# A graph network's kernel on one core: two reformulations, and new orders for three engines

## The chip, the core and the metric

The kernel runs on one core of a Trainium2 chip. A core has a matrix engine (TensorE, PE), three engines that work on 128 partitions at a time (VectorE, DVE; ScalarE, ACT; GpSimd, POOL) and SyncE (SP), which issues DMAs. They run side by side and wait for each other by semaphores; each takes its own instructions strictly in the order in which they were written. The metric is the device time of one execution in microseconds (us), as the median of several runs.

## What is computed

64 graphs of 128 nodes with 64 features; `adj` holds 0 and 1, with a self-loop at each node. Four layers follow one another, each with a residual and a layer norm:

```python
x = _layernorm(x + _L0_gnn_ref(x, adj, ...))   # PNA: mean, max, min, std over neighbours
x = _layernorm(x + _L1_gnn_ref(x, adj, ...))   # adj @ (x @ W) + bias
x = _layernorm(x + _L2_gnn_ref(x, adj, ...))   # weighted quantiles of the neighbours, then an MLP
x = _layernorm(x + _L3_gnn_ref(x, adj))        # (A @ x) / rowsum(A), A = adj + I
```

The parts that matter here:

```python
h_mod = h_cat @ W_pre + b_pre              # L0: a part of the node itself plus a part of the neighbour
mean = s1 / deg_safe
var = jax.nn.relu(s2 / deg_safe - mean * mean)
std = jnp.sqrt(var + EPS)
...
skip = jnp.where(m > T_THRESH, (m + K_DIL - 1) // K_DIL, 1)   # L2: drops some edges of rich nodes
sv = jnp.sort(vals, axis=2)                # L2: the neighbours' values, sorted for each feature
return y * mask[..., None].astype(dtp)     # L2; the mask is all ones in the inputs
...
num = jnp.einsum('bij,bjd->bid', A, nodes) # L3
denom = jnp.sum(A, axis=2, keepdims=True)
```

## The kernel before

The 64 graphs go through in eight groups of eight (`Turn`, `t.n` = 0 to 7). All steps of a group are small functions, each for one engine. What sets the order is written out by hand: TENSOR_ORDER, SCALAR_ORDER and VECTOR_ORDER are lists of entries `step:part@lag`, and `pipeline` goes through the list once per turn of the pipeline and runs each entry for group (turn + lag). So `so:0-20@-1` is the first 20 steps of the sort of the group before. In one turn up to three groups are at work, at different layers; with lags from -2 to 2 the loop makes ten turns that hold something, and the first and last hold little. A step starts when its semaphores (`s[...]`) allow it, and all that is queued behind it on its engine waits with it.

The steps of a group, in the order of the data (PE, ACT, DVE or POOL in brackets):

- Sorting the nodes of a graph by degree: `cm`, `gt`, `P` (DVE, P is a permutation matrix), `kc`, `lv` (PE). Permuting: `yr`, `ap`, `xt` (PE), evicted by `ysb`, `adj`, `xs` (ACT). `pb` copies P to bf16.
- `sm` (PE) fetches by P a table of per-node factors (`rows`, `rowsb`), and `rw` (DVE) adds up its three bf16 parts into `rowP`: 1/deg, deg/deg, two log-degree factors, 1/(deg+1) and 1 more, the mask. `kn`, `sk`, `dr`, `dt`, `dtc`, `va`, `vt`, `p1`, `k1`, `p2`, `k2`, `cr`, `sg` find which edges L2 drops, and number each node's neighbours (`key1` for L0, `key2` for L2).
- L0: `qp` (PE) makes the neighbour's part of `h_mod` in one half of PSUM tile `pna` and the node's own part in the other. `qo`, `pm`, `pl` (ACT) with `q1`, `q2` (PE) split the first into three bf16 parts, `ng` (DVE) negates them. `rp` and `up` (ACT) scale the node's own part by two factors, one instruction per graph each. `ss` (PE) multiplies by `adjP`, `ac` (ACT) scales by 1/deg. `me` (DVE) gives the mean with the node's part, `we` (DVE) the variance in four passes, `sd` the root, `mt` and `mts` a transpose. `h0` (DVE) makes one-hot matrices, `g0:0` to `g0:7` (PE) gather neighbours with them into a ring of two PSUM banks, `e0` (ACT) moves them out to `slot0`, `tr` (DVE) takes maxima and minima. `yl` (PE), `ys` (ACT), `zf` (DVE) make the layer's sum, and `n0q`, `n0d`, `n0r`, `n0x` the norm: squares (ACT), their sum (DVE), a root (ACT), the scaling (DVE). `n1..`, `n2..`, `n3..` do the same for the other layers.
- L1: `b1`, `b1e`, `b2`, `z1`, norm, result `x2`. `b3`, `b3e` transpose it.
- L2: `xh`, `xm`, `xl` (ACT) and `r1`, `r2` (DVE) split `x2` into three bf16 parts, `parts2`. `h2` (DVE) makes one-hot matrices, `g2:0` to `g2:3` (PE) gather through the same ring, `e2` (ACT) moves out to `slot2`. `so` (DVE) is a sorting network of 66 steps of minimum and maximum on `slot2` and `swap` (which the profile calls `hot`). `wr` (PE) makes the weights of the ranks, `wg` and `ag` (DVE) weigh and add the ranks; `c2` (PE), `c2e` (ACT), `c3` (PE) are the MLP, `y2e` (ACT) scales by the mask, graph by graph, `z2` (DVE) adds `x2`.
- L3: `c6` (PE) multiplies by `adjP`, `z3e` (ACT) scales by 1/(deg+1), `xr` (ACT) scales x3, `z3` (DVE) adds, and `sc` (POOL) scatters the rows to DRAM in eight indirect DMAs.

`pre` steps run once, in the first turns: degrees and factors, the weights, the tables, the rank weights. Where inputs are unusual, a slow general branch runs behind everything; with these inputs it does not.

Norms, matmuls and scalings all go through the helpers at L442, L445, L839 and L1440 to L1445, so many steps share these lines in the profile.

## Time and profile before

| | |
|---|---|
| median of 3 runs | 649.8 us (649.49 to 651.43) |
| the profiled execution | 646.34 us, its span 644.8 us |
| busy: VectorE | 514.6 us (80%) |
| busy: TensorE | 482.3 us (75%) |
| busy: ScalarE | 370.4 us (57%) |
| busy: GpSimd | 112.8 us (17%) |
| moved by DMA | 15.48 MB read, 2.10 MB written |

The shares are means over a start, five or six turns that repeat exactly, and an end in which little overlaps. A turn is best read by itself. In the timeline, a row is a start time, a length, an engine, a line of the kernel, and output and input by their names in the program; brackets give the idle time before it and whose work ended it.

### The profile page before, as it was taken

Reading aid. Unit: us, or ns where it says so; the run is one execution under the profiler, and the core shown is the slowest. Engines: PE = TensorE matmul, PEld = TensorE weight load, DVE = VectorE, ACT = ScalarE, POOL = GpSimd, SP = SyncE. Lnnn points to the kernel's source line nnn. Section 1 sums busy time; section 2 is a strip of 40 time slices with the busy share of each in tenths; the row PEclk is TensorE's granted clock in tenths of the full one; section 3 lists DMA queues with packets and bytes.
Section 4 is the critical chain, followed back from the end, with each engine's and each line's share of the span. In section 5 each row is a group of like instructions: output and inputs, shape, how many; then the busy total and the mean of one; then the engine's idle time right before and its main releaser. Section 6 shows DMA issues by size and latency. Waiting matters only on the chain.

```text
span 644.8 us, 10421 instructions
## 1 busy us (share of the span) xinstructions
PE 482.3 (75%) x3380; PEld 320.0 (50%) x3419; DVE 514.6 (80%) x1504; ACT 370.4 (57%) x990; POOL 112.8 (17%) x186
## 2 busy tenths in 40 slices
PE   2467968797988889798979897989888977861420
PEld 2443655365545655475557554755575545440220
DVE  4895639999799978999899989997999799379220
ACT  0264677447874678568855885588558842440230
POOL 4300010301014100510061006100610070006022
PEclk9866998999899989989998999899989997555555
DMA  8400020002000200020002000200000000000000
GB/s 312 162 0 1 2 82 1 2 1 82 2 4 16 81 2 2 17 83 2 2 16 83 2 1 18 83 2 1 17 2 2 2 17 2 1 0 17 0 6 15
DMA packets 6718, 18.32 MB, mean 28 GB/s; under 512 B 1792, under 2 KB 1920, under 8 KB 6144
## 3 DMA queue, kind: packets, MB, share of 16 engines
q1 hardware_dynamic: 4608, 15.48, 6.8%
q0 software_dynamic: 2048, 2.10, 1.1%
q8 instruction: 28, 0.46, 0.3%
q14 instruction: 34, 0.28, 0.1%
HBM read 15.48 MB, written 2.10 MB: 27 GB/s over the span
## 4 chain that ended last, share of the span: by engine, by line
DVE 34%; issue 27%; PE 22%; ACT 8%; POOL 6%; POOLq 0%; DVEq 0%; ACTq 0%
DVE hot L1479 7%; DVE slot L1479 7%; PE pna L445 6%; DVE slot L1404 5%; PE pna L442 5%; POOL out_dram L1099 5%; PE ring L442 4%; PE relab L442 2%; PE rest L442 2%; DVE deg L1143 1%; ACT wv L863 1%; PE ring L655 1%; DVE slot L1502 1%; DVE P L1309 1%; DVE hot L1492 1%
## 5 line engine op out<-in xcount | busy, mean ns | idle before, releaser
L442 PE MATMUL ring<-hot,parts 128*64 128x384 bf16 (+3 forms) x753 | 137.1, 358 | 0.9
L1099 POOL DMA_INDIRECT out_dram<-xo,idx x64 | 78.1, 1220 | 309.9 <-DVE xo L1445 292.9
L912 ACT ACTIVATE slot<-ring 128x512 f32<-128x512 f32 (+1 forms) x128 | 61.6, 525 | 42.6 <-PE ring L442 38.4
L442 PEld LDWEIGHTS ring<-hot,parts 128*128 128x128 bf16 (+1 forms) x768 | 55.5, 107 | 39.6 <-issue 4.1
L863 ACT ACTIVATE wv<-pna,rowP 128x64 f32<-128x64 f32 x128 | 28.0, 329 | 77.6 <-PE pna L442 77.6
L1404 DVE TENSOR_TENSOR slot<-slot 128x128 f32<-128x128 f32 (+2 forms) x144 | 53.1, 424 | 2.8 <-ACT slot L912 0.9
L1479 DVE TENSOR_TENSOR hot<-slot 128x64 f32<-128x64 f32 (+5 forms) x136 | 50.8, 407 | 3.5 <-ACT slot L921 3.5
L445 PE MATMUL ring<-emp,rowsel 112*128 112x512 bf16 (+1 forms) x128 | 45.3, 354 | 10.9 <-ACT slot L912 7.0
L1479 DVE TENSOR_TENSOR slot<-slot 128x64 f32<-128x64 f32 (+5 forms) x136 | 51.2, 406 | 0.0
L445 PE MATMUL pna<-bdx,xT 128*128 128x384 f32 x64 | 28.6, 530 | 16.5 <-DVE zF L1436 16.5
L921 ACT ACTIVATE slot<-ring 128x384 f32<-128x384 f32 x64 | 31.3, 502 | 15.3 <-PE ring L442 15.2
L442 PE MATMUL pna<-weights,QQ 128*128 128x192 f32 x128 | 36.6, 371 | 0.0
L445 PE MATMUL rest<-x2T,weights 128*128 128x512 f32 x32 | 22.3, 785 | 18.1 <-DVE x2T L1506 10.4
L442 PE MATMUL pna<-wmm,slot 128*128 128x192 f32 x128 | 34.5, 354 | 0.0
L1479 DVE TENSOR_TENSOR hot<-hot 128x128 f32<-128x128 f32 (+3 forms) x96 | 33.6, 378 | 0.0
L1085 POOL TENSOR_SCALAR skp<-dcol 128x2 f32<-128x2 f32 x8 | 2.1, 264 | 175.7 <-ACT dcol L780 175.7
L839 ACT ACTIVATE zB<-rest,rowP 128x64 f32<-128x64 f32 x128 | 28.0, 340 | 6.9 <-PE rest L442 4.0
L445 PE MATMUL ring<-sgnT,delta 32*128 32x512 bf16 (+2 forms) x48 | 14.6, 364 | 22.4 <-DVE slot L1492 20.3
L1479 DVE TENSOR_TENSOR slot<-hot 128x64 f32<-128x64 f32 (+5 forms) x88 | 31.3, 378 | 0.0
L1440 DVE TENSOR_REDUCE stB<-sqB 128x8 f32<-128x512 f32 x16 | 10.9, 683 | 25.2 <-ACT sqB L926 25.2
L445 PEld LDWEIGHTS ring<-emp,rowsel 112*128 112x128 bf16 x128 | 12.9, 101 | 33.8 <-ACT slot L912 22.2
L839 ACT ACTIVATE m<-pna,rowP 128x64 f32<-128x64 f32 x128 | 28.7, 394 | 0.1
(280 smaller groups left out, 1139.1 us busy)
## 6 DMA issues: line engine op xcount, KB each, us to landing
Cc<-adj_cols_dram SPq DMA_DIRECT2D x8, 512.0 KB, 3.8
R<-adj_rows_dram SPq DMA_DIRECT2D x8, 512.0 KB, 5.4
slot<-adj_rows_dram SPq DMA_DIRECT2D x4, 1024.0 KB, 12.4
xn<-x_nat_dram SPq DMA_DIRECT2D x8, 256.0 KB, 5.5
out_dram<-xo,idx POOLq DMA_INDIRECT x64
weights<-wpack_dram SPq DMA_DIRECT2D x1, 608.5 KB, 8.0
biasr<-wrows_dram SPq DMA_DIRECT2D x1, 128.0 KB, 9.4
own_loop<-adj_diag_dram SPq DMA_DIRECT2D x1, 32.0 KB, 15.1
```

Of the source, the lines that this page charges most:

```text
L442: return mm(*a, start=False, stop=True, skip_group_check=True, **k)
L445: return mm(*a, start=True, stop=True, skip_group_check=True, **k)
L655: mm(ps[:, OFF2[k] - lo:OFF2[k] - lo + CAP2[k]], fill2[:, k, :, :].rearrange("p a d -> p (a d)"), sgnT[t.n % KEEP][:, c, 0:CAP2[k]], start ...
L839: last = A(dst[:, g, :], src(g), ACT.Copy, scale=rowP[t.n % ROWKEEP][:, g, which:which + 1])
L863: last = A(ys[:, g, f, :], PQ[:, 256 * g + D * (f + 1):256 * g + D * (f + 2)], ACT.Copy, scale=rowP[t.n % ROWKEEP][:, 4 * h + g, AMP + f:A ...
L912: A(slot0[:, g, lo:hi], PG[ring["g0", t.n, 2 * g + j][0]][:, 0:hi - lo], ACT.Copy).then_inc(s["slot0"], 1)
L921: A(slot2[:, c, lo:hi], PG[ring["g2", t.n, 2 * c + j][0]][:, 0:hi - lo], ACT.Copy).then_inc(s["slot2"], 1)
L1099: nc.gpsimd.indirect_dma_start(out=out, out_offset=bass.IndirectOffsetOnAxis(ap=idx[t.n % ROWKEEP][:, g:g + 1], axis=0), in_=xo[:, g, :], ...
L1143: own(V.tensor_reduce(deg[:, k * CHUNK:(k + 1) * CHUNK], chunk[k], AX.X, ALU.add))
L1404: return V.tensor_tensor(dst, dst, src, ALU.max)
L1440: V.tensor_reduce(st[:, 0, :], sq[:, :, :], AX.X, ALU.add).then_inc(s[signal], 1)
L1479: mark(("sort", k), V.tensor_tensor(low if is_min else wire(b, 1 - sb_, width), low, high, ALU.min if is_min else ALU.max))
```

## The change

First reformulation, L0: the variance of `h_mod` over the neighbours does not depend on the node's own part. So in the normal path `qp` makes the neighbours' part only, `rp`, `up` and `me` are gone, and `we` is one subtraction. The own part of mean and maxima reaches the result through the weights `bdx`, which get one more product (`x_weights`, once). The mask goes the same way: `y2e` is gone, the one-column products with `maskb` in `sm` are gone, and an incomplete mask counts as unusual.

Second reformulation: L3 is multiplied by (deg + 1), which a norm cancels if its epsilon is scaled too: `z3e` is gone, `xr` scales by deg + 2, and `n3d` adds a correction `EPS3` to the sum of squares. `z2_` and `z3_` read PSUM directly. The table of factors has five columns where it had eight. And the three parts of `x2` are no longer rounded but cut: the upper 16 bits of each f32 word are used in place as bf16, at a step of two elements (`upper`), so `xh`, `xm`, `xl` are gone and `r1`, `r2` write `less[0]`, `less[1]`.

Third, the three orders are new. The list of VectorE is turned round, so that a turn begins with `wg:1`; most new lags come from that. Really moved are: steps 0 to 47 of the sort stand together; `z3` and `n3d`, `n3x` come late in the turn, with `c6` as `c6@-3` in TensorE's next turn; `va` and `p2` no longer stand between the `g2`; `rank_weights` (`pre:3`) comes after the degrees (`pre:4`); `adj` and `xs` end ScalarE's turn, `ac` comes before `e2:0`.

```diff
-INV, RATIO, AMP, ATT, RDEN, MASK, RDEN1, UNRATIO = range(8)
-NF = 8
-ROWW = 3 * NF + 1
+INV, AMP, ATT, DEG2, EPS3 = range(5)
+RATIO, UNRATIO, RDEN, RDEN1, MASK = range(3, 8)
+NF, GENERAL_NF = 5, 8
+ROWW, GENERAL_ROWW = 3 * NF + 1, 3 * GENERAL_NF + 1
+DEG_MAX = 1.0e9
...
-    g0:1@-1 cr@-1 g0:2@-1 g0:3@-1 kc@0 g0:4@-1 lv@0 g0:5@-1 g0:6@-1 g0:7@-1 yl:0@-1 wr:0@-2 wr:1@-2 yr@0 yl:1@-1
...
+    g0:1@-1 c6@-3 g0:2@-1 cr@-1 g0:3@-1 kc@0 g0:4@-1 g0:5@-1 g0:6@-1 lv@0 g0:7@-1 yl:0@-1 wr:0@-2 b3@-2 yr@0
...
-    adj@0 n0q@-1 xs@0 n0r@-1 kn@0 b3e@-2 qo@0 up@0 b1e@-1 rp@0 n1q@-1 c2e:0@-2 pm@0 n1r@-1 k1@0 xh@-1 pl@0
...
+    n0r@-1 qo@0 b1e@-1 kn@0 pm@0 c2e:0@-2 pl@0 n1q@-1 n1r@-1 c2e:1@-2 k1@0 ac@0 e2:0@-1 n2q@-2 e2:1@-1
...
-    zf:1@-1 wg:2@-2 nb@0 n0d@-1 wg:3@-2 pre:1@0 mp@0 n0x@-1 rw@0 wg:4@-2 wg:5@-2 ag@-2 z1@-1 dr@0 n1d@-1
...
+    h0:11-13@0 pre:4@0 pre:6@-2 cm@1 pre:3@0 so:0-47@-1 gt@1 so:47-50@-1 tr:0@0 so:50-53@-1 P@1 tr:1@0 z3@-2
...
+        def upper(words):
+            return words[:, :, :].bitcast(BF16).rearrange("p g (d two) -> p g d two", two=2)[:, :, :, 1]
+
+        def parts2(t):
+            return [upper(w) for w in (x2[t.n % 2], less[0], less[1])]
...
                 last.then_inc(s["q_ps"], 1)
-                for c in range(PAIRS):
-                    last = new(cols(bank(PQ, 1), c), xT[:, c, :], bdqp[:, 128:256])
-                last.then_inc(s["p_ps"], 1)
+                if not t.fast:
+                    for c in range(PAIRS):
+                        last = new(cols(bank(PQ, 1), c), xT[:, c, :], bdqp[:, 128:256])
...
-                            done = add(ps[64 * a:64 * a + 64, 0:hi - lo], parts2[:, 2 * c + a, part, :],
+                            done = add(ps[64 * a:64 * a + 64, 0:hi - lo], parts2(t)[part][:, 2 * c + a, :],
                                        hot2[:, 2 * c + a, lo:hi])
...
+            def x_weights(t):
+
+                pe.wait_ge(wdve, 1)
+                if t.fast:
+                    mm(PZ[:, 0:3 * D], wat, flat(raw[:, 6:9, :]), start=True, stop=False)
+                    mm(PZ[:, 0:3 * D], wat[0:64, :], flat(raw[0:64, 3:6, :]), start=False, stop=True).then_inc(vps, 1)
+                else:
+                    mm(PZ[:, 0:3 * D], wat, flat(raw[:, 6:9, :]), start=True, stop=True).then_inc(vps, 1)
...
-            def xh(t):
-                act.wait_ge(s["x2"], given(t))
-                before(act, "g2_ps", t, 1, 2 * PAIRS)
-                A(parts2[:, :, 0, :], x2[t.n % 2][:, :, :], ACT.Copy).then_inc(s["xh"], 1)
-
-            def xm(t):
-                act.wait_ge(s["xd1"], given(t))
-                A(parts2[:, :, 1, :], rest[:, :, :], ACT.Copy).then_inc(s["xm"], 1)
-
-            def xl(t):
-                act.wait_ge(s["xd2"], given(t))
-                A(parts2[:, :, 2, :], rest[:, :, :], ACT.Copy).then_inc(s["parts2"], 1)
-
             def c2e(t, a):
...
             def we(t):
 
                 dve.wait_ge(s["acs"], given(t))
-                dve.wait_ge(s["up"], given(t))
-                before(dve, "std", t)
-                dve.wait_ge(s["mean"], given(t))
+                if t.fast:
+                    before(dve, "std", t)
+                    dve.wait_ge(s["asq"], given(t))
+                    V.tensor_tensor(wv[:, :, :], QQ[:, :, 1, :], sqF[:, :, :], ALU.subtract).then_inc(s["vv"], 1)
+                    return
+                dve.wait_ge(s["up"], late(t))
+                dve.wait_ge(s["mean"], late(t))
                 own(V.tensor_tensor(wv[:, :, :], m4[:, :, 0, :], QQ[:, :, 0, :], ALU.add))
                 own(V.tensor_tensor(wv[:, :, :], wv[:, :, :], up, ALU.mult))
                 own(V.tensor_tensor(wv[:, :, :], wv[:, :, :], QQ[:, :, 1, :], ALU.add))
...
             def r1(t):
-                dve.wait_ge(s["xh"], given(t))
-                before(dve, "parts2", t)
-                V.tensor_tensor(rest[:, :, :], x2[t.n % 2][:, :, :], parts2[:, :, 0, :], ALU.subtract).then_inc(s["xd1"], 1)
+                before(dve, "g2_ps", t, 1, 2 * PAIRS)
+                dve.wait_ge(s["x2"], given(t))
+                V.tensor_tensor(less[0][:, :, :], x2[t.n % 2][:, :, :], upper(x2[t.n % 2]), ALU.subtract).then_inc(s["xd1"], 1)
 
             def r2(t):
-                dve.wait_ge(s["xm"], given(t))
                 dve.wait_ge(s["xd1"], given(t))
-                V.tensor_tensor(rest[:, :, :], rest[:, :, :], parts2[:, :, 1, :], ALU.subtract).then_inc(s["xd2"], 1)
+                V.tensor_tensor(less[1][:, :, :], less[0][:, :, :], upper(less[0]), ALU.subtract).then_inc(s["parts2"], 1)
 
             def z2_(t):
-                dve.wait_ge(s["y2s"], given(t))
                 dve.wait_ge(s["x2"], given(t))
+                if t.fast:
+                    dve.wait_ge(s["y2_ps"], given(t))
+                    before(dve, "sq3", t)
+                    V.tensor_tensor(flat(zB[:, :, :]), PZ[:, 512:1024], flat(x2[t.n % 2][:, :, :]),
+                                    ALU.add).then_inc(s["z2"], 1)
+                    return
+                dve.wait_ge(s["y2s"], late(t))
...
             def z3_(t):
-                dve.wait_ge(s["z3s"], given(t))
                 dve.wait_ge(s["xr"], given(t))
+                if t.fast:
+                    dve.wait_ge(s["z3_ps"], given(t))
+                    V.tensor_tensor(flat(zB[:, :, :]), PZ[:, 512:1024], flat(xr[:, :, :]),
+                                    ALU.add).then_inc(s["z3"], 1)
+                    return
+                dve.wait_ge(s["z3s"], late(t))
                 V.tensor_tensor(zB[:, :, :], zB[:, :, :], xr[:, :, :], ALU.add).then_inc(s["z3"], 1)
 
             def n3d(t):
-                summed(t, stB, sqB, "sq3", "rd3")
+                if not t.fast:
+                    summed(t, stB, sqB, "sq3", "rd3")
+                    return
+                dve.wait_ge(s["sq3"], given(t))
+                own(V.tensor_reduce(stB[:, 0, :], sqB[:, :, :], AX.X, ALU.add))
+                V.tensor_tensor(stB[:, 0, :], stB[:, 0, :], row_of(t)[:, :, EPS3], ALU.add).then_inc(s["rd3"], 1)
 
```

TensorE, a middle turn, from the second bank of `g2:0` on (`fill` and `hot,parts` are `g2`, `maskP`, `dts` and `Pb` are `va`). Before:

```order
L442 MATMUL ring<-hot,parts 64x424 x6
L445 MATMUL relab<-maskP,identb 128x512
L442 MATMUL relab<-dts,Pb 128x32
L442 MATMUL relab<-Pb,dts 32x128
...
L655 MATMUL ring<-sgnT,fill 128x128 x3
L442 MATMUL ring<-hot,parts 64x384 x6
```

The same place now, and the end of `g2:3` further on:

```order
L456 MATMUL ring<-hot,less 64x424 x4
L676 MATMUL ring<-sgnT,fill 128x128 x3
L456 MATMUL ring<-hot,x_0 64x384 x2
...
L459 MATMUL relab<-identb,drop 128x128 x2
L459 MATMUL ring<-emp,rowsel 128x512
L456 MATMUL ring<-hot,parts 128x512 x3
L459 MATMUL ring<-emp,rowsel 128x328
L456 MATMUL ring<-hot,parts 128x328 x3
L459 MATMUL relab<-maskP,identb 128x512
```

`g2:1` follows `g2:0` at once, and `va` comes behind `dt` and `g0:0`.

ScalarE, a middle turn, from `ac` (QQ, then sqF) on; `slot<-ring` are the evictions `e2`, `zB` is `y2e`. Before:

```order
L887 ACTIVATE QQ<-pna,rowP 128x128 x8
L892 ACTIVATE sqF<-QQ 128x512
L921 ACTIVATE slot<-ring 128x384
L921 ACTIVATE slot<-ring 128x424
L839 ACTIVATE zB<-rest,rowP 128x64 x8
L796 ACTIVATE validT<-relab 128x1024
```

And now:

```order
L817 ACTIVATE key<-relab,not_member 128x1024
L914 ACTIVATE QQ<-pna,rowP 128x128 x8
L919 ACTIVATE sqF<-QQ 128x512
L948 ACTIVATE slot<-ring 128x384
L948 ACTIVATE slot<-ring 128x424
L953 ACTIVATE sqB<-zB 128x512
L948 ACTIVATE slot<-ring 128x384
L948 ACTIVATE slot<-ring 128x424
L957 ACTIVATE stB<-stB,eps 128x8
```

`y2e` and `vt` are gone from between the evictions, `n2q` (sqB) and `n2r` (stB) have moved up there.

VectorE, a middle turn, from the end of `ag` (x2T) on. Before:

```order
L1506 TENSOR_TENSOR x2T<-x2T,slot 128x512
L1457 TENSOR_TENSOR zF<-rest,x 128x512
L1344 TENSOR_SCALAR drop<-keyN,skp 128x128 x2
L1348 SCALAR_TENSOR_TENSOR drop<-keyN,skp,drop 128x128 x2
L1440 TENSOR_REDUCE stF<-sqF 128x8
```

That place in the turn shows this in the changed kernel:

```order
L1541 TENSOR_TENSOR x2T<-x2T,slot 128x512
L1353 TENSOR_SCALAR maskP<-adjP 128x1024
L1401 TENSOR_SCALAR hot<-key_0 128x8x128
L1363 TENSOR_REDUCE rowP<-relab 128x40
L1365 COPY nkS<-relab 112x1
L1366 TENSOR_TENSOR idx<-relab,base 128x8
L1401 TENSOR_SCALAR hot<-key_0 128x8x128 x2
L1492 TENSOR_TENSOR zF<-rest,x 128x512
```

`mp`, `rw` and the first one-hot matrices stand between `ag` and `z1`.

## Rows read from the trace of the kernel before

**Rows 1.** Busy time by stretch: start and end, length, engines, PEclk, DMA share, GB/s.

```profile
330.50:395.39 64.89, 55.89 (x424) 37.52 (x428) 59.17 (x171) 45.06 (x123) 11.92 (x18) 0.97 0.08 26
```

**Rows 2.** Timeline of VectorE in that turn: start, us, engine, line, operation.

```profile
330.50 1.22 DVE L1309 TENSOR_TENSOR P<-place,placed 128x1024 f32<-128x1024 f32 x1
...
345.98 0.42 DVE L1435 TENSOR_TENSOR zF<-pna,wv 128x256 f32<-128x256 f32 x1 [0.49 <-ACT wv L863]
...
351.29 0.72 DVE L1492 TENSOR_TENSOR hot<-hot,ring 128x288 f32<-128x288 f32 x2 [0.41 <-PE ring L445]
...
355.55 0.69 DVE L1506 TENSOR_TENSOR x2T<-x2T,slot 128x512 f32<-128x512 f32 x1
...
373.81 0.69 DVE L1440 TENSOR_REDUCE stB<-sqB 128x8 f32<-128x512 f32 x1 [3.61 <-ACT sqB L926]
...
376.76 0.22 DVE L1479 TENSOR_TENSOR hot<-slot 128x64 f32<-128x64 f32 x1
```

**Rows 3.** Timeline of TensorE in that turn: c2, c2, ss, g2, va, g2, c6.

```profile
356.30 1.13 PE L445 MATMUL rest<-x2T,weights 128*128 128x512 f32 x2 [0.94 <-DVE x2T L1506]
358.40 1.10 PE L445 MATMUL rest<-x2T,weights 128*128 128x512 f32 x2 [0.98 <-ACT hT L984]
...
360.98 2.05 PE L445 MATMUL pna<-QQ,adjP 128*128 128x128 f32 x16 [0.82 <-ACT parts L835]
...
364.92 0.34 PE L655 MATMUL ring<-sgnT,fill 32*128 32x128 bf16 x3
...
366.79 0.39 PE L445 MATMUL relab<-maskP,identb 128*128 128x512 bf16 x1
...
369.48 0.34 PE L655 MATMUL ring<-sgnT,fill 32*128 32x128 bf16 x3
...
376.08 2.00 PE L445 MATMUL rest<-x,adjP 128*128 128x64 f32 x16
```

**Rows 4.** Timeline of ScalarE in that turn: ac, and the last eviction of g2.

```profile
363.32 2.16 ACT L887 ACTIVATE QQ<-pna,rowP 128x128 f32<-128x128 f32 x8
...
375.74 0.98 ACT L921 ACTIVATE slot<-ring 128x384 f32<-128x384 f32 x2
```

**Rows 5.** Groups over the run: busy us, mean ns, idle before.

```profile
L839 ACT ACTIVATE m<-pna,rowP 128x64 f32<-128x64 f32 x128 | 28.7, 394 | 0.1
...
L839 ACT ACTIVATE zB<-rest,rowP 128x64 f32<-128x64 f32 x128 | 28.0, 340 | 6.9 <-PE rest L442 4.0 <-PE rest L445 2.9
...
L445 PE MATMUL pna<-weights,xT 128*128 128x128 f32 x64 | 9.3, 293 | 0.0
...
L1391 DVE TENSOR_TENSOR wv<-wv,m 128x512 f32<-128x512 f32 x8 | 5.5, 692 | 0.3
```

**Rows 6.** Groups by form, weight loads of TensorE with 64 columns.

```profile
L442 PEld LDWEIGHTS ring<-hot,parts 128*64 128x64 bf16 x384 | 17.2, 114 | 9.0 <-issue 1.5 <-DVE hot L1370 0.2
...
L445 PEld LDWEIGHTS rest<-adjP,x 128*64 128x64 f32 x128 | 7.5, 147 | 1.3 <-DVE x L1445 1.0
```

**Rows 7.** Timeline of the start, VectorE three times (rank_weights, h0, sort), TensorE (g0:1).

```profile
38.98 0.29 DVE L1263 TENSOR_SCALAR zB<-steps_of 32x2 f32<-32x2 f32 x3
...
42.88 2.33 DVE L1362 TENSOR_SCALAR hot<-key 128x1024 bf16<-128x1024 bf16 x9
...
57.84 0.39 PE L445 MATMUL ring<-emp,rowsel 112*128 112x512 bf16 x1 [2.98 <-ACT slot L912]
...
114.33 0.91 DVE L1479 TENSOR_TENSOR hot<-slot 128x64 f32<-128x64 f32 x1 [1.13 <-ACT slot L921]
```

**Rows 8.** Timeline of the end: two sorts begin, c6 of TensorE, z3e of ScalarE.

```profile
506.52 0.23 DVE L1479 TENSOR_TENSOR hot<-slot 128x64 f32<-128x64 f32 x1 [0.36 <-ACT slot L921]
...
569.32 3.68 PE L445 MATMUL rest<-x,adjP 128*128 128x64 f32 x16
...
569.99 0.23 DVE L1479 TENSOR_TENSOR hot<-slot 128x64 f32<-128x64 f32 x1 [2.01 <-ACT slot L921]
...
618.58 1.75 ACT L839 ACTIVATE zB<-rest,rowP 128x64 f32<-128x64 f32 x8 [1.72 <-PE rest L445]
```

193 lines of the change are left out of this document (112 added, 81 removed).

## The prediction

> **What bounds the kernel now.** First the busy time by engine in one turn of the pipeline [rows 1]: of 64.89 us VectorE is busy for 59.17, TensorE for 55.89, ScalarE for 45.06. VectorE is the bound, but it stands still for 5.7 us of each turn, so the next question is where. Its own instructions in order of time [rows 2] answer that: 3.61 us before the reduction of `sqB` at 373.81, 0.49 before `zF`, 0.41 before the weighting at 351.29, and small change of some 0.1 us each. The 3.61 us lie in one stretch. It begins when `ag` has finished (355.55 and 0.69, so 356.24) and ends with the first step of the sort at 376.76: 20.52 us, in which VectorE works for 16.9.
>
> What fills the 20.52 us is seen on TensorE and ScalarE [rows 3, 4]. `c2` starts at 356.30 and again at 358.40, `ss` (the product with `adjP`) runs from 360.98, `c3` behind it, `g2:0` starts at 364.92. The four `g2` would take 1.87 each, but `va` stands between the first two from 366.79 to 369.48, and the last ends at 376.08. ScalarE moves its last half out at 375.74 to 376.72, and the sort starts. So the critical path runs through ag, c2, ss, c3, g2 with va in it, and the evictions, and back to VectorE.
>
> **Change, part 1: work taken away.** ScalarE, per graph group: `rp` and `up` are 16 instructions of the 128 that take 28.7 us, so 3.6 us; `y2e` and `z3e` are the 128 that take 28.0 us, 3.5 us [rows 5]; the three casts `xh`, `xm`, `xl` some 0.6 each (the size of a 512-wide pass), 1.8 us. ScalarE falls from 45.06 to some 36.2 us. It is not the bound, and 28 us of the turn cover it; this pays only where its queue held others up.
>
> VectorE: `me` goes and so do three of the four passes of `we`. One pass is 0.69 alone [rows 5], 0.60 behind another one, and 0.72 where it waits for its own predecessor: 0.60 + 3 x 0.72 = 2.76 us off. `rw` is narrower, 0.1 off. Added: `n3d` gets one 128x8 addition and a wait on its own reduction, 0.25 on. `z2_` and `z3_` now read PSUM where they read `zB`; nothing in the rows prices a PSUM operand apart, so between nothing and 0.1 each; I take nothing. Sum: 2.6 us.
>
> TensorE: the second half of `qp` goes, 9.3 us for 64 instructions, 1.16 with overlap, 1.0 net [rows 5], and eight one-column products with `maskb`, some 0.1. From 55.89 to some 54.7 us. The one matmul that `x_weights` adds runs once, below 1 us.
>
> `parts2` is now the upper half of each f32 word of `x2` and `less`, so the weights of `g2` are bf16 at a step of two elements. No row shows such a load. The nearest from below is the packed 64-column bf16 load, 114 ns; from above the 64-column f32 load, 147 ns [rows 6]. Below zero is excluded, since the same number of columns is loaded. There are 48 such loads per turn: 0 to 48 x 0.033 = 1.6 us, all on the path above. I take 0, since the matmuls behind these loads hide part of them. The Trainium skill ("SBUF — State Buffer", the note on cachelines) says that bf16 can be read at a step within a 16-byte line without loss if a line serves at least two reads; by it the price is 0 too, and no run here shows it yet. VectorE reads the same strided halves in `r1` and `r2`; before, it read bf16 there as well, so no change.
>
> **Change, part 2: the new orders.** In the stretch from ag to sort, counted from the end of ag: VectorE keeps its 16.9 us of work, less 2.76, plus `mp` and `rw` that moved in behind `ag` (0.6 and 0.5), less some small waits: 15.0 us. The path of TensorE: `c2:0` 1.16; `c2e:0` is hidden behind `q2` and `p1`, which now stand between the two `c2`, so that `c2:1` starts at 2.2 and ends at 3.3; `ss` then takes 2.05 (to 5.4), and `c3` 1.85 (to 7.25) (360.98 to 364.92 for both [rows 3]). `c3` needs `c2e:1`, which ScalarE now issues only behind `n1q` and `n1r`, so behind z1 and n1d on VectorE: 5.1, just in time. `g2:0` starts at 7.25 and ends at 9.1. Here the order costs something: `ac` (8 scalings and a square, 2.7 us, [rows 4]) stands ahead of `e2:0`, and starts behind `k1` at 6.05, so the first eviction comes at 8.8 and `g2:1` waits 0.2. Then `n2q` (0.6) and `n2r` stand between evictions; `n2r` waits for `n2d` on VectorE, at 12.5, while the ring has but two banks. The four `g2` end at 15.2 and not at 14.7, the last eviction at 15.7. `va`, `mt` and `p2` are gone from between the `g2` and come behind `g0:0`, where TensorE has 4 us of slack per turn. So the stretch falls from 20.5 to 15.7, and VectorE still waits 0.7 us in it.
>
> The rest of the turn was 64.89 - 20.52 = 44.4 us, with 0.9 of waits [rows 2]. Less `mp` and `rw` 1.1, plus 0.25, less 0.1, it is 42.6 without waits. The sort now runs in one piece of 47 steps with nothing in it, then alternates with `gt`, `tr`, `P`, `z3`, `zf`. Followed one by one, what VectorE meets there: `kc` is done about 0.3 us before `gt`; `lv` 1.2 before `P`; the last `e0` 4 before `tr:1`; `ys:0` 0.6 before `zf:0`; `ys:1`, which now stands behind `n3r` and so behind `n3d`, 0.9 before `zf:1`. No big wait, but thin margins; I put 0.6 us for them, within the 0 to 0.9 that such waits cost before. A turn is then 42.6 + 0.6 + 15.7 = 58.9 us.
>
> **Sum over the run.** The sorts start at 114.33 for the first group, at 376.76 for the fifth, 506.52 for the seventh and 569.99 for the last [rows 2, 7, 8]. From the first to the fifth that is 65.6 per turn, later 64.88: the early turns are a little longer, and on the mean of six, 65.37, 0.5 above the steady one. I take 0.3 for it: 59.2 x 6 = 355.2.
> Start: `g0:1` begins at 57.84 [rows 7], held by ScalarE's first eviction, which waits for the degrees of the later graphs. `rank_weights`, 38.98 to 42.88, now comes behind those degrees, and 2.8 us of `me` and `we` are gone; TensorE then has its own work (`va`, `mt`, `p2` at a low clock) until some 53.5, so 4.3 us come off. The half turn that follows, from the end of the second `zf` (345.98 and its two passes, 346.8 [rows 2]) to the sort, falls from 30.0 to 23: 9.4 to 7.2 for the part up to ag, since `nb`, `mp`, `rw` and a weighting lie elsewhere, and 20.5 to 15.7. First sort: 114.3 - 4.3 - 7.0 = 103.
> The last interval was 63.5 us, with TensorE at half clock [rows 8], and its path (ag, c2, c3, g2) has neither `va` nor `ss` in it before or after: 63.5 kept.
> End: 644.8 - 569.99 = 74.8 us from the last sort, one chain without overlap. In it `y2e` and `z3e`, 1.75 us each [rows 8], are gone, 0.25 is added: 71.5. `c6` and `z3` a turn later add nothing there, since nothing else is left to do.
> 103 + 355.2 + 63.5 + 71.5 = 593.2 us of span, with the 1.5 around it 594.7 for a profiled execution (646.3 before). The median of the runs lies 0.54% above the profiled one (649.8 to 646.34): 597.9, so 598.
>
> **Rivals.**
> *A, VectorE without waits.* If the evictions keep up better than I walked, the stretch is VectorE's own 15.0 and the thin margins hold: 57.6 + 0.3 per turn, so 8 us less and up to 4 at the start: 586. For it: the walk adds waits of ScalarE's queue one behind another. Against: the order `ac` ahead of `e2:0` is fixed.
> *B, strided weights cost.* 1.6 us per turn on the path, times 8: 598 + 13 = 611. For it: f32 loads of the same width take 147 against 114 ns. Against: loads overlap matmuls (PEld is busy 37.5 of 64.9 us).
> *C, the order gives less than it says.* If the thin margins fail (a late `ys:1`, `gt` or `P`), half of the waits come back at another place. With all the waits that were (4.5 us) the turn is 59.2 - 2.6 + 0.7 + 4.5 = 61.8: 598 + 6 x 2.9 = 615; nothing but the removed work counts then.
> *D, slower.* One mechanism: TensorE's clock. Over the steady turn the granted clock is 0.97 [rows 1]; in the last 100 us the records show the lower level, 1.2 GHz, and the same 16 instructions of `c6` take 3.68 where they took 2.00 [rows 3, 8]. If the new order left pauses in which the clock falls, TensorE's 54.7 us would grow by up to 0.84 of themselves; slower than before begins where more than a quarter of its work is at the lower level (54.7 x 1.21 = 66). All at that level would be 100 us a turn, 850 us. Against: TensorE will be busy for 93% of the turn, more than now.
>
> **Chances.** The forecast (590 to 606) 0.55, A 0.15, B 0.10, C 0.16, D 0.02, and 0.02 that it all cancels within 0.3%, which is about what a measurement of this kernel can tell from no change. Faster by over 0.3%: 0.96; same 0.02; slower 0.02. The likeliest is 598. The range takes in A (586) with 2 us below it and C (615) with 2 above: 584 to 617.
>
> **What would show it.** Right: turns of 58.5 to 59.5 us between two sorts; VectorE's wait before the sort under 1.5 us, behind ScalarE's `slot`; ScalarE busy for 36 us of a turn, VectorE for 56.6; first sort near 103; the four `g2` in one run of some 8 us. B shows as weight loads of `parts2` longer than 114 ns, C as new waits before `gt`, `P` or `zf`. The prediction is wrong first if the ring of two banks holds `g2` longer than 8 us, or if the start does not move.

## The result, and the profile after

The changed kernel takes 587.9 us (median of four executions: 579.32, 587.55, 588.17 and 589.48), the kernel before 649.6 us beside it. Every ratio in this document leaves out executions that took over 1.5% more than the fastest one of their kernel, which here leaves 579.32 and 587.55, in the mean 583.4 us. The ratio is 0.898, with a 95% interval of 0.887 to 0.909; in a second measurement it is 0.902 (0.895 to 0.908). The direction was right and the size was not: 52 us were forecast to be saved, the medians save 62, these two executions 66 in the mean and the shortest one 70.

The profiled execution is the one of 589.48 us, the longest of the four. What of it an execution of 579.66 us shows too, and what not, is in the first experiment. These are its stretches: a steady turn, the part of it from the end of `ag` to the sort, the last interval between two sorts, and the end. The columns are the stretch, its length, the busy time (and instructions) of TensorE, its weight loads, VectorE, ScalarE and GpSimd, then the granted clock of TensorE, the share of the DMA engines and GB/s.

```profile
core 0: us, PE busy (x) PEld busy (x) DVE busy (x) ACT busy (x) POOL busy (x), PEclk, DMA share, GB/s
277.11:335.11 58.00, 54.00 (x413) 35.41 (x411) 56.22 (x168) 37.57 (x89) 10.16 (x16) 1.00 0.09 29
319.45:335.11 15.66, 15.14 (x138) 9.12 (x138) 14.52 (x46) 10.96 (x26) 2.96 (x10) 1.00 0.02 6
451.14:516.92 65.78, 56.23 (x307) 33.18 (x305) 47.60 (x137) 27.96 (x68) 7.86 (x8) 0.75 0.02 5
516.92:587.20 70.28, 19.29 (x66) 12.62 (x65) 34.36 (x103) 8.66 (x25) 15.39 (x16) 0.50 0.03 8
```

The turn is 58.00 where it was 64.89 [rows 1]; VectorE is busy for 56.22 us of it. So of the 6.9 us per turn 3.0 are work that VectorE no longer does (59.17 to 56.22) and 3.9 are time in which it no longer stands still (5.7 to 1.8). What it still waits for is seen in its rows in order of time. In one whole turn there is one wait of more than 0.05 us (in brackets, us of idle time and who ended it):

```profile
318.75 0.69 DVE L1541 TENSOR_TENSOR x2T<-x2T,slot 128x512 f32<-128x512 f32 x1
...
333.56 0.69 DVE L1319 TENSOR_SCALAR key<-Cc 128x1024 bf16<-128x1024 f32 x1
335.11 0.23 DVE L1514 TENSOR_TENSOR hot<-slot 128x64 f32<-128x64 f32 x1 [0.86 <-ACT slot L948]
```

The first row is the last pass of `ag`, the third the first step of the sort. The waits of 3.61, 0.49 and 0.41 us [rows 2] are gone; 0.86 is left. TensorE and ScalarE in that stretch, to be laid beside [rows 3, 4]:

```profile
319.50 1.12 PE L459 MATMUL rest<-x2T,weights 128*128 128x512 f32 x2
...
321.61 1.10 PE L459 MATMUL rest<-x2T,weights 128*128 128x512 f32 x2
322.54 1.95 PE L459 MATMUL pna<-QQ,adjP 128*128 128x128 f32 x16
324.43 0.39 PE L459 MATMUL rest<-biasb,rows 128*128 128x512 bf16 x1
...
326.48 0.34 PE L676 MATMUL ring<-sgnT,fill 32*128 32x128 bf16 x3
...
332.56 0.34 PE L676 MATMUL ring<-sgnT,fill 32*128 32x128 bf16 x3 [0.19 <-ACT slot L948]
...
334.45 0.28 PE L459 MATMUL relab<-identb,drop 128*128 128x128 bf16 x2
```

```profile
325.27 2.17 ACT L914 ACTIVATE QQ<-pna,rowP 128x128 f32<-128x128 f32 x8
327.48 0.63 ACT L919 ACTIVATE sqF<-QQ 128x512 f32<-128x512 f32 x1
328.02 0.98 ACT L948 ACTIVATE slot<-ring 128x384 f32<-128x384 f32 x2
...
334.56 0.52 ACT L948 ACTIVATE slot<-ring 128x424 f32<-128x424 f32 x1 [0.51 <-PE ring L456]
```

`c2`, `c2`, `ss`, `c3` follow each other without a pause, the four `g2` run from 326.48 to 334.45 in one piece, and the last half is moved out at 334.56 to 335.08. The stretch is 15.66 us.

### The profile page after: what moved, and what is told of

It reads as the page before. It is cut to its first block, busy times and chain, and to the rows that moved or that the text cites. A ratio compares the mean times of both kernels' runs of the same rounds, so it can differ in the third digit from the quotient of the medians.

```text
span 587.2 us, 9826 instructions
## 1 busy us (share of the span) xinstructions
PE 470.0 (80%) x3293; PEld 305.9 (52%) x3293; DVE 490.4 (84%) x1480; ACT 308.2 (52%) x710; POOL 96.3 (16%) x179
## 4 chain that ended last, share of the span: by engine, by line
issue 63%; POOL 14%; DVE 10%; PE 8%; ACT 2%; POOLq 0%; DVEq 0%; ACTq 0%
POOL out_dram L1115 11%; PE pna L456 2%; PE ring L456 2%; DVE slot L1514 1%; DVE hot L1514 1%; PE pna L459 1%; PE ring L459 1%; ACT wv L892 1%; PE relab L459 1%; DVE hot L1393 1%; DVE slot L1439 1%; PE relab L456 0%; DVE biasb L1228 0%; DVE deg L1157 0%; DVE pcol L1257 0%
## 5 line engine op out<-in xcount | busy, mean ns | idle before, releaser
L1115 POOL DMA_INDIRECT out_dram<-xo,idx x64 | 64.9, 1014 | 353.6 <-DVE xo L1480 336.6
L456 PE MATMUL ring<-hot,parts 128*128 128x512 bf16 (+1 forms) x384 | 90.1, 347 | 0.0
L939 ACT ACTIVATE slot<-ring 128x512 f32<-128x512 f32 (+1 forms) x128 | 62.7, 522 | 36.2 <-PE ring L456 36.1
L456 PEld LDWEIGHTS ring<-hot,parts 128*128 128x128 bf16 x384 | 38.0, 99 | 30.2 <-issue 1.9
L456 PE MATMUL ring<-hot,less 128*64 128x384 bf16 (+1 forms) x256 | 35.5, 360 | 0.0
L456 PE MATMUL pna<-weights,m 128*128 128x192 f32 x128 | 34.4, 351 | 0.0
L456 PE MATMUL pna<-wmm,slot 128*128 128x192 f32 x128 | 32.3, 335 | 0.0
L676 PEld LDWEIGHTS ring<-sgnT,fill 32*128 32x128 bf16 x352 | 16.3, 95 | 25.4 <-ACT slot L948 12.5
L676 PE MATMUL ring<-sgnT,fill 32*128 32x128 bf16 (+5 forms) x352 | 25.1, 198 | 3.9 <-DVE less L1565 2.0
L456 PEld LDWEIGHTS pna<-weights,m 128*128 128x128 f32 x128 | 22.0, 199 | 7.7 <-issue 7.7
```

What stands on the lines that cost most here:

```text
L456: return mm(*a, start=False, stop=True, skip_group_check=True, **k)
L676: mm(ps[:, OFF2[k] - lo:OFF2[k] - lo + CAP2[k]], fill2[:, k, :, :].rearrange("p a d -> p (a d)"), sgnT[t.n % KEEP][:, c, 0:CAP2[k]], start ...
L939: A(slot0[:, g, lo:hi], PG[ring["g0", t.n, 2 * g + j][0]][:, 0:hi - lo], ACT.Copy).then_inc(s["slot0"], 1)
L1115: nc.gpsimd.indirect_dma_start(out=out, out_offset=bass.IndirectOffsetOnAxis(ap=idx[t.n % ROWKEEP][:, g:g + 1], axis=0), in_=xo[:, g, :], ...
```

## Experiments

Each is one edit of the changed kernel; `work_only` has three order tables edited, nearly back to those of the kernel before. "The changed kernel" is 588 us in the median, with turns of 58.0.

**The same kernel again** (after_again).

> The changed kernel itself once more, for its spread: four executions gave 579.32, 587.55, 588.17 and 589.48 us, with mean granted clocks of 0.915, 0.897, 0.894 and 0.886. Theory 1: the spread is TensorE's clock in the last 100 us alone; the turns between the sorts stay at 58.0 us in every execution, and an execution with a clock of 0.91 or more comes out near 579, one with 0.89 near 588. Theory 2: the steady turns differ as well (58.0 against some 57.0), and then an execution near 579 shows first sort and end as in the 587.2 us span. A median between 579 and 588 is expected by both.

Measured: 579.66 to 590.44 us, median 588.3. The profiled execution was one of 579.66:

```profile
217.75:275.74 57.99, 53.50 (x407) 35.42 (x411) 56.22 (x168) 37.54 (x89) 10.14 (x16) 1.00 0.08 28
449.73:507.04 57.31, 47.24 (x307) 29.74 (x308) 47.66 (x138) 27.72 (x68) 8.04 (x8) 0.91 0.02 6
```

The steady turn is the same to 0.01 us, and the end to 0.02 (70.26). The last interval is 57.31 in place of 65.78, with a clock of 0.91 in place of 0.75. That is 8.5 of the 9.9 us between the two spans (587.2 and 577.3); 1.3 more lie ahead of the second sort, which starts at 161.09 and 159.75. Theory 1 holds for most of the spread: it is one interval, in which TensorE's clock holds or does not. Only two executions of this kernel were profiled. A third length is in c6_early and n2_late below, whose turns are those of this kernel too: 63.58 us (in an execution of 586.77) and 63.24 (587.39). The first:

```profile
450.74:514.32 63.58, 53.18 (x303) 31.60 (x306) 47.47 (x138) 27.80 (x68) 8.62 (x8) 0.81 0.02 5
```

**The removed work alone** (work_only). Order tables as in the kernel before, without the steps that are gone. The larger part of ScalarE's:

```
-    ... qo@0 up@0 b1e@-1 rp@0 n1q@-1 ... k1@0 xh@-1 pl@0 c2e:1@-2 xm@-1 dtc@0 xl@-1 ac@0 e2:0@-1 y2e@-2 vt@0 ...
+    ... qo@0 b1e@-1 n1q@-1 ... k1@0 pl@0 c2e:1@-2 dtc@0 ac@0 e2:0@-1 vt@0 ...
```

> Only the removed work: all that the change takes away or reformulates is gone, but the steps of TensorE, ScalarE and VectorE stand in the order of the kernel before. Theory 1 (the orders carry the larger part, as the prediction's sum had it): VectorE's 2.6 us per turn go and part of its 4.5 us of waits stays, since va and p2 still stand between the g2: turns of 61 to 62.3 us, a time of 618 to 628 us. Theory 2 (ScalarE's queue was what held the evictions up, so its 8.9 us free the path by themselves): waits go too, turns of 58.5 to 59.5, 598 to 605 us.

Measured: 636.3 us (ratio 0.981, interval 0.976 to 0.986). Both theories expected more of a saving. Its sorts start at 110.20, 172.06, 240.21, 304.13, 370.41, 434.32, 500.63 and 563.8: 4.1 us less in the start, 0.3 per turn (65.07 in the mean, 65.37 before), 4.3 less in the end. Two of its turns:

```profile
370.41:434.32 63.91, 55.08 (x408) 36.28 (x413) 56.29 (x170) 37.28 (x89) 11.72 (x16) 0.97 0.08 26
434.32:500.63 66.31, 57.41 (x408) 37.47 (x413) 55.86 (x169) 37.40 (x89) 11.72 (x16) 0.92 0.02 5
```

VectorE is busy for 56.3 us as in the changed kernel, ScalarE for 37.3, and from the third on the turns alternate between 64 and 66 (the first two take 61.9 and 68.2). The time is in one wait, which was 3.61 [rows 2] and is 6.24 in the shorter turns and 6.48 in the longer, as here, and in ScalarE's queue ahead of it:

```profile
367.46 0.69 DVE L1477 TENSOR_REDUCE stB<-sqB 128x8 f32<-128x512 f32 x1 [6.48 <-ACT sqB L955]
```

```profile
363.23 1.02 ACT L830 ACTIVATE validT<-relab 128x1024 bf16<-128x1024 f32 x1 [2.16 <-PE relab L458]
...
366.82 0.61 ACT L955 ACTIVATE sqB<-zB 128x512 f32<-128x512 f32 x1
```

`sqB` stands behind `vt` (`validT`), and `vt` waits for `va` on TensorE. VectorE comes 2.6 us earlier to the same door. The turns with the clock of the kernel before, 0.97, are 63.91 where they were 64.89: the removed work is worth 1.0 us there. The others, at 0.92, give it back. Nearly all of their 2.4 us more is in `c2:1` and `ss`. The two `c2` in a short turn, then in a long one:

```profile
284.24 1.13 PE L461 MATMUL rest<-x2T,weights 128*128 128x512 f32 x2 [1.89 <-DVE x2T L1543]
286.35 1.10 PE L461 MATMUL rest<-x2T,weights 128*128 128x512 f32 x2 [0.98 <-ACT hT L1000]
...
348.16 1.23 PE L461 MATMUL rest<-x2T,weights 128*128 128x512 f32 x2 [1.89 <-DVE x2T L1543]
350.37 2.05 PE L461 MATMUL rest<-x2T,weights 128*128 128x512 f32 x2 [0.98 <-ACT hT L1000]
```

The waits are the same to 0.01 us in both turns, and only in the second does the clock fall. So the small saving is the work of the queue and of the clock together.

**va and p2 back between the g2** (va_back).

```
-    ... ss@0 c3@-2 g2:0@-1 g2:1@-1 g2:2@-1 g2:3@-1 dt@0 g0:0@0 va@0 mt@0 p2@0
+    ... ss@0 c3@-2 dt@0 g2:0@-1 va@0 g2:1@-1 p2@0 g2:2@-1 g2:3@-1 g0:0@0 mt@0
-    ... ac@0 e2:0@-1 n2q@-2 e2:1@-1 n2r@-2 e2:2@-1 e2:3@-1 pre:0@2 dtc@0 sd@0 xr@-2 vt@0 ...
+    ... ac@0 dtc@0 e2:0@-1 n2q@-2 vt@0 e2:1@-1 n2r@-2 e2:2@-1 e2:3@-1 pre:0@2 sd@0 xr@-2 ...
```

> The changed kernel with one move undone: va stands again between the first two g2 and p2 between the next two, dt ahead of g2:0, and ScalarE's dtc and vt where they feed them. Theory 1 (the path from ag to the sort is TensorE's): va was 2.7 us there, p2 about 1, so the stretch from ag to the sort grows from 15.6 to 18.5 to 19.5 us, the turn from 58.0 to 61 to 62, the time by 18 to 24 us. Theory 2 (VectorE's work alone sets the turn, and TensorE has slack): under 1 us per turn, within 6 us of the changed kernel.

Measured: 619.31, 625.49, 635.88 and 651.60 us, with mean clocks of 0.887, 0.870, 0.854 and 0.818. Two turns of the execution of 625.49:

```profile
172.61:234.65 62.04, 53.65 (x407) 35.37 (x411) 56.32 (x168) 37.63 (x89) 10.13 (x16) 1.00 0.08 27
234.65:300.49 65.84, 57.29 (x407) 36.18 (x411) 56.35 (x168) 37.74 (x89) 10.15 (x16) 0.92 0.08 25
284.00:291.00 7.00, 5.71 (x42) 2.77 (x42) 5.95 (x20) 3.41 (x9) 0.00 (x0) 0.69 0.00 0
```

At full clock the turn is 62.04, 4.0 more, the top of what theory 1 gave, and the stretch from ag to the sort holds all of it (19.70 us where it was 15.66). The longer turns have the same work at a lower clock, from the first `g2` on, which costs 3.8 us more per turn. The span of 623.3 us is 36 longer than that of the changed kernel, where theory 1 had 18 to 24: 29 lie in the six turns (24 of it at 4.0 each), 10 ahead of the first sort, and the last interval is 3 shorter. Ahead of those `g2`, `dt` waits for VectorE's `drop`, but the rows of a short turn (the first) and of a long one show the same wait:

```profile
223.02 0.27 PE L459 MATMUL relab<-identb,drop 128*128 128x128 bf16 x2 [0.95 <-DVE drop L1379]
...
285.04 0.27 PE L459 MATMUL relab<-identb,drop 128*128 128x128 bf16 x2 [0.95 <-DVE drop L1379]
```

So the wait alone does not tell in which turn the clock falls. The two longest executions were not profiled.

**ac and the norms later on ScalarE** (ac_late), and **the norms alone** (n2_late).

```
-    ... ac@0 e2:0@-1 n2q@-2 e2:1@-1 n2r@-2 e2:2@-1 e2:3@-1 ...
+    ... e2:0@-1 ac@0 e2:1@-1 n2q@-2 e2:2@-1 n2r@-2 e2:3@-1 ...      (ac_late)
+    ... ac@0 e2:0@-1 e2:1@-1 n2q@-2 e2:2@-1 n2r@-2 e2:3@-1 ...      (n2_late)
```

> The changed kernel with ScalarE's ac behind the first eviction of g2 and n2q, n2r one eviction later each. Theory 1 (the prediction's walk: ac ahead of e2:0 and the norms between the evictions make VectorE's last wait, 0.86 us before the sort): the wait falls to 0 to 0.3 us, turns of 57.2 to 57.7, 2 to 5 us less in all. Theory 2 (g2 itself, 1.9 to 2.1 us for each of four, sets the end of the stretch): nothing within 1 us. Theory 3: the weighted mean and deviation come later and hold yl up: 0.5 us or more per turn longer.

> The changed kernel with n2q and n2r one eviction later each on ScalarE; ac stays ahead of the first eviction. It parts the two moves of the run with both, which took 61.2 us per turn: there VectorE waited 2.1 us for the square of ac and 0.4 for the root of n2. Theory 1 (the cost was ac's): turns within 0.3 us of 58.0, the time within 3 us of the changed kernel. Theory 2 (the norms between the evictions are what counts): turns of 59.5 to 61, 9 to 18 us more.

Measured: 609.5 us (ratio 0.942, 0.938 to 0.945) and 587.0 us (0.902, 0.896 to 0.908). With `ac` later the turn is 61.22, theory 3. Its waits:

```profile
340.65 0.69 DVE L1421 TENSOR_TENSOR wv<-QQ,sqF 128x512 f32<-128x512 f32 x1 [2.10 <-ACT sqF L919]
...
343.79 0.20 DVE L1479 RECIPROCAL stB<-stB 128x8 f32<-128x8 f32 x1 [0.41 <-ACT stB L957]
...
346.72 0.23 DVE L1514 TENSOR_TENSOR hot<-slot 128x64 f32<-128x64 f32 x1 [1.00 <-ACT slot L948]
```

VectorE's `we` needs the square behind `ac`; the wait before the sort that the move was to remove grew to 1.00. With the norms alone moved, the wait before the sort is gone, 0.40 and 0.35 us stand before two steps of the norm instead, and the turn is 57.99 as before. So the prediction was right that `ac` ahead of `e2:0` puts the first eviction off (it starts at 328.02, as soon as `ac` is done, without a wait for TensorE), but the price of the other order is higher; and the 0.86 us cannot be had on ScalarE by this shift of the norms.

**VectorE's removed time put back** (dve_back): four passes ahead of `we`.

```
+                    for _ in range(4):
+                        own(V.tensor_tensor(junk[:, :, :], QQ[:, :, 1, :], sqF[:, :, :], ALU.subtract))
                     V.tensor_tensor(wv[:, :, :], QQ[:, :, 1, :], sqF[:, :, :], ALU.subtract).then_inc(s["vv"], 1)
```

> The changed kernel with VectorE's removed time put back where it was, ahead of the pass of we: four passes over 128x512 f32 (no result of theirs is used), each waited for by VectorE itself, some 0.72 us each, 2.9 us per graph group. Theory 1 (with the new orders VectorE's own work is the turn): the 0.86 us of wait before the sort take up a part, the rest goes into the turn: 2.0 to 2.9 us for each of 6 turns and for the first, none in the last interval, so 14 to 20 us more than the changed kernel, turns of 60 to 60.9. Theory 2 (TensorE's path from ag to the sort is the turn): under 1 us per turn, under 7 us in all.

Measured: 615.2 us (ratio 0.948, 0.944 to 0.952), so 27 us more. A turn and the second half of its stretch, and the added passes:

```profile
291.30:352.77 61.47, 55.37 (x413) 35.90 (x412) 59.02 (x173) 37.54 (x89) 10.14 (x16) 0.97 0.08 27
343.00:352.77 9.77, 6.66 (x72) 3.32 (x71) 8.10 (x23) 3.88 (x10) 0.00 (x0) 0.90 0.01 2
```

```profile
343.90 2.86 DVE L1423 TENSOR_TENSOR junk<-QQ,sqF 128x512 f32<-128x512 f32 x4
...
352.77 0.23 DVE L1517 TENSOR_TENSOR hot<-slot 128x64 f32<-128x64 f32 x1 [1.40 <-ACT slot L949]
```

2.86 us of VectorE make the turn 3.47 longer: the size of theory 1, and more than it. But the 0.86 us of wait took nothing up; it grew to 1.40. The way leads through the other two engines:

```profile
348.95 0.30 ACT L958 ACTIVATE stB<-stB,eps 128x8 f32<-128x8 f32 x1 [3.69 <-DVE stB L1478]
...
349.68 0.34 PE L677 MATMUL ring<-sgnT,fill 32*128 32x128 bf16 x3 [3.11 <-ACT slot L949]
```

The first row is `n2r`, which stands between two evictions and now waits 3.69 us for `n2d` on VectorE (0.77 in the changed kernel). The last `g2` waits behind that eviction, 3.11 us where it was 0.19, and starts 16.0 us after the end of `ag` where it was 13.1. That is 2.9 of the 3.5 us. The other 0.5 is the clock, 0.70 from the start of that `g2` to the sort.

**Time put back on ScalarE** (act_back): 16 small copies ahead of n1q, 3 wide ones ahead of ac, 8 small ones behind e2:0 and 8 behind e0:0.

```
-    ... pl@0 n1q@-1 n1r@-1 c2e:1@-2 k1@0 ac@0 e2:0@-1 n2q@-2 ... vt@0 e0:0@0 ...
+    ... pl@0 extra:0@0 n1q@-1 n1r@-1 c2e:1@-2 k1@0 extra:3@0 extra:3@0 extra:3@0 ac@0 e2:0@-1 extra:1@0 n2q@-2
+        ... vt@0 e0:0@0 extra:1@0 ...
```

> The changed kernel with ScalarE's removed time put back near where it was (32 copies of 64 columns and 3 of 512 to a scratch buffer, no result of theirs used): 16 small ones ahead of n1q, the 3 wide ones between k1 and ac, 8 small ones behind e2:0 and 8 behind e0:0; some 8.9 us per graph group. Theory 1 (ScalarE is no bound, its work is covered): under 1 us per turn. Theory 2 (its queue holds up what VectorE waits for, in the place where it stands): 16 ahead of n1q make n1 3.6 us late and so c2e:1, c3 and g2, and the 1.8 us ahead of ac as well: 3 to 6 us per turn, 20 to 40 us in all.

Measured: 638.5 us (ratio 0.983, 0.978 to 0.988), so 50 us more, beyond theory 2. ScalarE is busy for 43.55 us of a turn (6.0 us more, less than the 8.9 put down), far from being the bound, and the turn is 64.79, as long as in the kernel before:

```profile
303.62:368.41 64.79, 58.12 (x413) 36.85 (x412) 56.62 (x169) 43.55 (x124) 10.15 (x16) 0.92 0.08 26
357.00:368.41 11.41, 9.57 (x73) 4.40 (x74) 5.86 (x20) 6.99 (x23) 0.00 (x0) 0.62 0.01 1
```

Three of the added groups stand in the stretch from ag to the sort, with 2.44, 1.95 and 1.27 us, 5.7 together. TensorE's rows show how they become 6.8 us of turn:

```profile
352.89 0.39 PE L460 MATMUL rest<-biasb,rows 128*128 128x512 bf16 x1 [1.88 <-ACT hT L999]
...
358.84 0.34 PE L677 MATMUL ring<-sgnT,fill 32*128 32x128 bf16 x3 [1.95 <-ACT slot L949]
...
361.31 0.49 PE L677 MATMUL ring<-sgnT,fill 32*128 32x128 bf16 x3
...
364.53 0.49 PE L677 MATMUL ring<-sgnT,fill 32*128 32x128 bf16 x3
```

`c3` waits 1.88 us and the second `g2` 1.95 us for ScalarE. Then the clock falls within that `g2`, and the last two take 3.2 us each (361.31 to 364.53 to 367.74) in place of 2.0. Here the waits and the slower products behind them add up.

This run does not have the old work in its old place. In the kernel before, `up` and `rp` ran ahead of the end of `ag` at 356.24 [rows 2], and `n1q` still waited 1.43 us for VectorE behind them:

```profile
351.56 1.76 ACT L839 ACTIVATE m<-pna,rowP 128x64 f32<-128x64 f32 x8
353.61 1.84 ACT L839 ACTIVATE m<-pna,rowP 128x64 f32<-128x64 f32 x8
```

Here the 16 copies start 2.3 us after the end of `ag` (348.25 and 345.97) and hold `n1q` up. So the run prices ScalarE's time in this place of the new order, and does not show what the new orders would give with the old work where it was.

**rank_weights early** (ranks_early).

```
-    ... n1x@-1 h2:8-9@-1 ... pre:6@-2 cm@1 pre:3@0 so:0-47@-1 ...
+    ... n1x@-1 pre:3@0 h2:8-9@-1 ... pre:6@-2 cm@1 so:0-47@-1 ...
```

> The changed kernel with rank_weights (3.9 us of VectorE, once) again ahead of the degrees of the later graphs, everything else as it is. Theory 1 (the start is held by the degrees, which release ScalarE's first eviction): the degrees end at 53.3 in place of 49.4, g0:1 starts at 53.8 to 54.9 in place of 51.0, the first sort some 3 to 3.9 us later, and the time 3 to 4 us longer. Theory 2 (TensorE's own work until 51.0 us holds it in the changed kernel): 2 us or less.

Measured: 592.7 us (ratio 0.912, 0.907 to 0.917), some 4 to 5 us more. ScalarE's first eviction starts at 52.84 where it started at 49.66, and the second `g0` at 54.16 where it started at 50.99, 3.2 later, as theory 1 had it for the step; the first sort is 7 us later (108.05), the second 4.9. The rest of the 7 us lies in 90 to 108 us, where the clock is 0.73 and 0.50 and was 1.00 in the changed kernel:

```profile
90.00:100.00 10.00, 7.71 (x60) 4.47 (x60) 9.66 (x34) 6.49 (x16) 0.77 (x4) 0.73 0.00 0
100.00:108.00 8.00, 8.00 (x55) 3.38 (x53) 3.48 (x12) 2.54 (x6) 4.62 (x5) 0.50 0.00 0
```

So the step itself moves 3.2 us. Whether the clock fell behind it because of the move, one profiled execution does not show.

**c6 a turn earlier** (c6_early).

```
-    g0:1@-1 c6@-3 g0:2@-1 ... g2:3@-1 dt@0 g0:0@0
+    g0:1@-1 g0:2@-1 ... g2:3@-1 c6@-2 dt@0 g0:0@0
```

> The changed kernel with c6 back behind the last g2 of the turn before (lag 2 in place of 3), all else as it is; z3 and its norm stay where they are on VectorE and ScalarE. Theory 1 (a turn later costs nothing, and c6 ahead of dt, g0:0, va, mt and p2 delays these by 1.9 us, within TensorE's slack): turn 58.0, no difference over 1 us. Theory 2 (the start of g0 sets when the last halves of the slots are there for tr and zf): 1 to 2 us per turn, 6 to 12 us in all.

Measured: 587.4 us (ratio 0.903, 0.897 to 0.908), turn 58.01: no difference, theory 1. The last layer's place on TensorE, taken alone, is worth nothing.

**TensorE kept busy** (warm_last, warm_end, warm_tuned). A step that issues products without use, in the last graph group only:

```
+            def hot(t, k):
+                if t.n == NG - 1:
+                    pe.wait_ge(s["sgnT"], given(t))
+                    for _ in range(k):
+                        nc.tensor.matmul(PT[:, 512:1024], identb[:, :], onesb[:, :], start=True, stop=True, ...)
```

> The changed kernel with 33 products more in the last interval alone (no result of theirs is used: 128x512 bf16 into the PSUM of the relabelling, which is free by then), put ahead of the instructions of TensorE that wait there: 8 ahead of yl:1, 2 and 2 and 4 between the wr, 7 ahead of b1, 3 ahead of b2, 4 ahead of c2:1, 3 ahead of c3. Theory 1 (the spread from 579 to 590 us, and the 65.8 us of the last interval, are TensorE at 1.2 GHz after it stood waiting): with the engine busy the clock holds, the last interval is 57 to 58 us in every execution, all times lie at 577 to 581 us, and the executions near 588 are gone. Theory 2 (the clock falls whatever TensorE does there): last interval 66 to 68, times of 588 to 592, the added products only in the way.

> As the one before, and the same kind of product after the last sort has begun: 60 ahead of the first fill that waits, 4 and 2 between the fills, 20 ahead of c2:0, 4 ahead of c2:1, 3 ahead of c3, 26 ahead of c6, all in the last graph group. Theory 1: in the end, 70.3 us at the lower clock, c2 twice, c3 and c6 are on the path with 2.07, 2.05, 3.5 and 3.67 us; at full clock they took 1.16, 1.15, 1.85 and 2.0: 5.1 us less, so 572 to 576 us. Theory 2: nothing of it, or the added products stand in front of the ones that are waited for: 579 to 585.

> The run before with added products to the end, their numbers set by its trace: 24 more between the first two fills, where TensorE stood for 5.9 us and fell to 1.2 GHz, 2 in place of 4 ahead of the next, 14 in place of 26 ahead of c6, where they were 1.7 us in the way; the rest as it was. Theory 1 (the end is on the path with c2, c3 and c6, and the added products stood in front of them by some 2 + 1.7 us, and 1.2 us at the fills): the end from the last sort falls from 69.5 to 65 to 67.5 us, the time to 572 to 574.5 us. Theory 2 (the end does not hang on TensorE's clock): the end stays at 69.5 and the time at 576.

Measured: warm_last 577.05 to 580.29 us (six executions, ratio 0.891), warm_end 576.2 (0.887), warm_tuned 571.2 (0.882, interval 0.878 to 0.886), 17 us below the changed kernel's median and better than both kernels. The last interval of warm_last is 54.57 us at full clock, below the 57 to 58 expected; the execution of 579.66 us had part of it at the lower clock:

```profile
451.35:505.92 54.57, 51.61 (x343) 29.60 (x341) 47.28 (x138) 27.83 (x68) 8.63 (x8) 1.00 0.02 6
```

In warm_end the added products stood in front of `c2` and `c6`, and the end gave 69.5 us; with their numbers set to the gaps it is 64.5 (warm_tuned):

```profile
504.32:568.80 64.48, 38.66 (x188) 18.96 (x191) 34.34 (x103) 8.66 (x25) 15.91 (x16) 0.84 0.03 9
```

```profile
543.42 2.00 PE L459 MATMUL rest<-x,adjP 128*128 128x64 f32 x16 [0.65 <-DVE x L1487]
```

`c6` takes 2.00 us there, as in the turn; in the end of the changed kernel it took 3.67, and 3.68 near the end of the kernel before [rows 8].

## Why the prediction was right or wrong

Its sum against the changed kernel's profiled span, and against the second profiled execution:

| term | predicted | 589.48 us | 579.66 us |
|---|---|---|---|
| first sort | 103 | 100.9 | 101.75 |
| six turns | 355.2 (59.2) | 350.2 (58.4) | 348.0 (58.0) |
| last interval | 63.5 | 65.8 | 57.3 |
| end | 71.5 | 70.3 | 70.3 |
| outside the span | 1.5 | 2.3 | 2.4 |

- **The stretch from ag to the sort: right.** 15.7 us were walked, 15.66 measured. `c2:1` at 2.2, `ss` to 5.0, `g2:0` from 7.0, first eviction at 8.6 and the last half out at 15.6 us after the end of `ag` are the walk to within half a microsecond. VectorE's wait was put at 0.7, and is 0.86; its own work in the stretch was put at 15.0 and is 14.5. Rival A, which had the wait gone, is wrong as to the place.
- **The rest of the turn: the failing term of the turns.** 42.6 without waits and 0.6 of waits at thin margins were put, and 58.00 - 15.66 = 42.34 measured. The 0.6 us is not there at all: VectorE starts `gt`, `P`, `tr`, `zf` without any wait. `kc` is ready 1.3 us ahead of `gt`, `lv` 2.0 ahead of `P`, `ys:0` 1.6 ahead of `zf:0`, `ys:1` 0.5 ahead of `zf:1`. With 0.3 us off the work and 0.6 of waits that did not come, the steady turn is 0.9 below 58.9, which makes 5.4 us over six turns. The 0.3 on top for the early turns (65.8 and 66.9 us before, where only the four behind them are alike) came out as 0.4 in one execution, with a first turn of 60.2, and as nothing in the other. Of rival A the half on the margins is what came true; that its 586 us lies nearer to the result than 598 is luck, since its other half, a stretch of 15.0 us, is not there.
- **Work removed: sizes right, meaning wrong.** VectorE is busy for 56.2 (56.6 said), TensorE for 54.0 (54.7), ScalarE for 37.6 (36.2 said: the 35 instructions that are gone took 45.06 - 37.57 = 7.5 us and not 8.9, since neighbours overlap a little, as 327.48 with its 0.63 us and 328.02 do above). `z2_` and `z3_` take 0.68 to 0.69 us with an operand in PSUM, as they did with `zB`, so to take nothing for them was right. But the sentence that ScalarE's saving "pays only where its queue held others up" left its price out. Beside each other, the mean of the six turns in us: the kernel before 65.4; old orders and the work gone 65.1 (work_only); new orders with 2.86 us put back on VectorE 61.8 (dve_back); new orders with 6.0 us put back on ScalarE, 5.7 of it in the stretch from ag to the sort, 65.0 (act_back); both new 58.4. The removed work without the orders gives 0.3 us per turn, or 1.0 in the turns with no more clock lost than before, and with the orders there are 7.0. What the orders give without the removed work was not run: the two runs that put time back put it into places of the new order, and part of what they cost is clock (0.97 and 0.92 in their turns, 1.00 in the changed kernel).
- **Strided weights: right.** The profile's rows for `g2`'s loads: 114 ns for the packed ones before [rows 6], and now

```profile
L456 PEld LDWEIGHTS ring<-hot,less 128*64 128x64 bf16 x256 | 15.4, 117 | 4.4 <-issue 0.7
L456 PEld LDWEIGHTS ring<-hot,x 128*64 128x64 bf16 x128 | 7.3, 110 | 4.5 <-issue 0.8
```

  The mean is (256 x 117 + 128 x 110) / 384 = 115 ns, so rival B is refuted. By the Trainium skill ("SBUF — State Buffer", the note on cachelines) no loss was to be expected at this step; the trace agrees, 115 to 114 ns.
- **Start: mis-sized by 2.** The second `g0` starts 6.9 us earlier (57.84 [rows 7], now 50.99), not 4.3: TensorE's own work behind `g0:0` (`dt`, `va`, `mt`) was said to last until 53.5 and ends at 51.0, with ScalarE's first eviction already at 49.66. The half turn behind it gave 6.5 of the 7.0. In ranks_early, with `rank_weights` ahead of the degrees again, the degrees put the eviction and the second `g0` off by 3.2 us; in the changed kernel TensorE's own work is what ends last, by under 1 us.
- **The last interval, "63.5 kept": the other failing term.** It was taken as a constant of the program. It is not: the same kernel takes 65.8 or 57.3 us there, c6_early 63.6, and warm_last 54.6 where TensorE is kept busy. The step that failed was to carry the row's clock over as if it were part of the path's price. For the executions near 579 us this is 6.2 us of what was missed; in the one of 589.48 it went the other way by 2.3. Executions near 587 may have had just the 63.5: c6_early and n2_late had 63.6 and 63.2 there, but none of this kernel near 587 was profiled.
- **End: right** to 1.2 us.
- **From the profiled execution to the median: wrong in sign.** The median before lay 0.54% above its profiled execution; here the profiled execution lies above its median, 589.48 to 587.9. That correction added 3.3 us to the forecast and moved it away from the result; where an execution of the changed kernel lies hangs for the most part on the last interval's clock.
- **Rival C and rival D.** No waits came back before `gt`, `P` or `zf`. The clock did not fall in the turns, but rival D's mechanism is real nearby: in va_back turns with the same work took 62.04 us at a clock of 1.00 and 65.84 at 0.92, and act_back had its last two `g2` at the lower level. The changed kernel has a clock of 1.00 in its turns, where it was 0.97 [rows 1]; the sum did not have this, and no run prices it alone.

Sorted by size, the profiled execution came out 5.2 us below the predicted 594.7: turns 5.0, start 2.1 and end 1.2 below, the last interval 2.3 and the time outside the span 0.8 above. The scaling to the median adds 3.3, and the difference of profiled execution and median 1.6; that makes the 10 us between 598 and 587.9. In the execution of 579.66 us it is 15.0: turns 7.2, last interval 6.2, start 1.2 and end 1.2 below, the time outside the span 0.8 above; with the 3.3 of the scaling that is 18 us below 598. All of it but the last interval and the time outside the span went the same way, so that 598 was too high for every execution. The mechanism of the saving (the way from ag to the sort shortened, and work taken from VectorE) was right; the waits in the rest of the turn, the fixed last interval and the scaling were not.

What stays open: which single one of the moved steps gives the most. Two were undone alone; `c6` is worth nothing, and va, p2 and what feeds them are worth 4.0 us per turn at full clock. What lets the clock fall in one turn and not in another with the same waits is open too. The sort in one piece was not tried by itself, and neither was the interleaving of `q2` and `p1` with `c2`.

## What to carry to other kernels

When three engines hand work around in a ring, work taken from one of them can buy little until the order lets the next one start earlier (here 0.3 to 1.0 us of 2.9 per turn), so price a removal together with the queue that stands behind it, and test both halves alone. Where a path's instructions run at a lower TensorE clock, do not carry their price over as fixed: look at what the engine waited for just before, and profile more than one execution, since a wait there can cost the wait and slower products behind it, and not in every turn. If a drain phase leaves TensorE with gaps, products without use that just fill the gaps can pay, and too many of them stand in the way.

## What the runs showed of the hardware

- TensorE's granted clock went to the lower level (1.2 GHz) in products that stood behind waits of 1 to 2 us for other engines: 2.08 us for `x` in the last interval of the changed kernel, 1.95 us in act_back, 1.89 and 0.98 in every second turn of work_only. The four `g2` take 8.0 us at 2.4 GHz in a turn and 12.9 at 1.2 in the last interval.
- The same waits do not always do it, not even within one execution: in work_only and va_back one turn at the lower clock and one without stand behind waits equal to 0.01 us. Between executions, behind nearly the same waits in the last interval, the clock was back for the `g2` in one (57.31 us) and not in another (65.78). With the gaps filled all six executions lay within 3.2 us, where six of the changed kernel lay within 10.8.
- 33 added products of 128x512 bf16 in the last interval cost nothing that could be seen: it took 54.57 us with them, and without them 57.31, 63.58 (c6_early) and 65.78.
- Weights of 64 columns in bf16, read at a step of two elements, load in 115 ns, packed in 114 (changed kernel and kernel before).
